# Index operations in halves, one row-blend batch, a near search to distance 5, and half of one sweep's search by VectorE's maxima

## The reference

```
center = einsum('nchw,oc->nohw', feature, w_center)          # 2 channels
step   = relu(einsum('nchw,oc->nohw', feature, w_step))      # 2 channels
prob   = sigmoid(einsum('nchw,oc->nohw', feature, w_prob))   # 1 channel
offset = center * step
th = minimum(round(gh + offset[0]), h - 1); tw = minimum(round(gw + offset[1]), w - 1)
tgt    = mod(th * w + tw, h * w)
sample = grid.at[tgt].set(grid)       # scatter: the last pixel that aims at a target wins
sampled = bilinear sample of feature at sample's coordinates (on whole pixels up to rounding)
proped = sampled * prob + feature * (1 - prob)
out    = feature * prob + proped * (1 - prob)
```

## The kernel before

| sweep | mixing | tabling | indices |
|---|---|---|---|
| 0 | | 0 | |
| 1 | | 1 | 0 |
| 2 | 0 | 2 | 1 |
| 3 | 1 | 3 | 2 |
| 4 | 2 | | 3 |
| 5 | 3 | | |

## Time and profile before

### The profile page before, as it was taken

One profiled execution on the slowest core, in us unless ns is written; L12 is line 12 of the kernel. 1 busy time (PEld: TensorE's weight loads), 2 busy tenths in 40 slices (PEclk: granted clock), 3 DMA queues, 4 the chain that ended last, 5 costly groups with the idle time before them and its releaser, 6 DMA issues. The chain is left out here.

```text
span 8694.0 us, 95812 instructions
## 1 busy us (share of the span) xinstructions
PE 6551.5 (75%) x26980; PEld 3016.8 (35%) x26980; DVE 5132.8 (59%) x11678; ACT 3770.3 (43%) x7426; POOL 4294.5 (49%) x8828
## 2 busy tenths in 40 slices
PE   5885675557657899579996787679996774688888
PEld 2332232223223444234552333234442332233333
DVE  3333355355754433555558885477778982566666
ACT  5664434323223444233330233456661654455555
POOL 3556866444343345443431443564452644566665
PEclk8997788768878999789999888789998786788888
DMA  4785545755456677555551377665551554676676
GB/s 177 285 296 185 201 167 203 193 175 191 143 142 213 243 281 277 188 183 188 196 207 60 136 240 217 204 178 177 177 179 53 177 176 121 191 221 221 217 222 200
DMA packets 489245, 1673.92 MB, mean 193 GB/s; under 512 B 119580, under 2 KB 140347, under 8 KB 421396
## 3 DMA queue, kind: packets, MB, share of 16 engines
q1 hardware_dynamic: 214092, 827.29, 30.9%
q10 hardware_dynamic: 210152, 764.05, 23.0%
q0 software_dynamic: 64480, 76.57, 4.8%
HBM read 949.99 MB, written 727.71 MB: 193 GB/s over the span
## 5 line engine op out<-in xcount | busy, mean ns | idle before, releaser
L1056 DVE TENSOR_TENSOR ps<-ps,arena 128x400 f32<-128x400 f32 x1600 | 928.4, 580 | 2178.1 <-PE ps L1170 1058.7
L1006 POOL TENSOR_TENSOR arena<-arena 128x32 f32<-128x32 f32 (+8 forms) x3358 | 968.8, 329 | 2497.4 <-PE ps L1193 1752.4
L1162 PE MATMUL ps<-arena,minus 128*128 128x400 f32 x3200 | 1692.4, 614 | 484.5 <-DVE arena L1058 359.0
L1318 ACT ACTIVATE arena<-ps 128x400 f32<-128x400 f32 x1600 | 800.8, 501 | 2584.7 <-PE ps L1156 968.5
L1193 PE MATMUL ps<-arena,w_conv 128*10 128x400 f32 x3200 | 1367.7, 535 | 284.1 <-ACT arena L1252 114.0
L1206 PE MATMUL ps<-ident,arena 128*128 128x128 f32 x5000 | 870.6, 320 | 615.6 <-ACT arena L1268 370.2
L1136 POOL DMA_INDIRECT arena<-table,gidx x800 | 903.8, 1130 | 829.4 <-PE ps L1179 570.0
L1252 ACT ACTIVATE arena<-ps 10x400 f32<-10x400 f32 x1600 | 785.2, 492 | 1119.2 <-PE ps L1193 1004.6
L1268 ACT ACTIVATE arena<-ps 128x512 f32<-128x512 f32 (+1 forms) x1400 | 731.8, 550 | 914.8 <-PE ps L1206 671.2
L1170 PEld LDWEIGHTS ps<-ident,arena 100*128 100x128 f32 x6400 | 779.6, 155 | 797.4 <-issue 643.4
L1136 POOL DMA_INDIRECT arena<-table,arena x800 | 810.0, 1013 | 480.0 <-issue 233.7
(11 more groups left out here) (210 smaller groups left out, 6313.6 us busy)
## 6 DMA issues: line engine op xcount, KB each, us to landing
arena<-x SPq DMA_DIRECT2D x200, 1600.0 KB
arena<-table SPq DMA_DIRECT2D x400, 800.0 KB
table<-arena ACTq DMA_DIRECT2D x400, 512.0 KB
y<-arena ACTq DMA_DIRECT2D x100, 1600.0 KB, 14.2
arena<-y SPq DMA_DIRECT2D x100, 1600.0 KB
out<-arena ACTq DMA_DIRECT2D x100, 1600.0 KB
table<-arena ACTq DMA_DIRECT2D x200, 576.0 KB
conv<-arena ACTq DMA_DIRECT2D x800, 31.2 KB
```

What stands on the lines that cost most here:

```text
L1006: last = E.tensor_tensor(tmp[:, :, at:at + size], cols[:, :, y + to:end + to:step], cols[:, :, y:end:step], ALU.subtract)
L1056: V.tensor_tensor(d, d, g, ALU.mult).then_inc(s_mix, 1)
L1162: nc.tensor.matmul(ps[:, 4 + r % 2, 0:W], minus[:, :], tile(t)[:, r * W:(r + 1) * W], start=True, stop=False)
L1318: nc.scalar.activation(gate[r % 2], ps[:, 6 + r % GB, 0:W], ACT.Copy).then_inc(s_gcopy, 1)
```

## The change

Four things are changed, and the paces with them.

1. *Halves.* In sweeps that mix (2, 3, 4) each whole-map piece of parts (1) and (4) becomes two pieces on 1600 elements (`pieces`, `cuts` = 2). Sweep 1 keeps whole pieces.
2. *Batches.* NEARBY becomes a list by tabled unit: 8 for units 0 and 1, tabled in sweeps 0 and 1, and 4 for units 2 and 3. With 8, no tile has two batches.
3. *Distance.* R of layer 1 is 5 and not 6: 121 offsets in place of 169.
4. *Search of unit 2 (sweep 3).* TensorE's sum is formed for two of the four row pairs only. For the other two VectorE compares into a float16 value i + 1 and takes the maximum with the running result in SBUF. Each step is one `found`, one compare for the other half and one maximum, two steps to a piece (`held` = 2).
5. *Pace* becomes 1.15 in sweeps 3 and 4, so about every seventh slot takes two pieces.

```diff
-NEARBY = 4
+NEARBY = [8, 8, 4, 4]
-REACH = [1, 6]
+REACH = [1, 5]
...
-        htmp = [part(W) for _ in range(NEARBY)]
+        htmp = [part(W) for _ in range(NEARBY[-1])]
...
+        htmp += [again(gates_at[0] - (a + 1) * W, W) for a in range(2)] + gate
...
+            PAIRED, held = (2, 2) if u == 2 else (BROWS // 2, HELD)
+            beside = [again(BPX // 2 + a * W, 2 * W, NB, F16).rearrange("p (r w) -> p r w", w=W) for a in range(2)]
...
+                def pieces(op, name=None):
+
+                    for a in range(cuts):
+                        size = BROWS // cuts
+                        note(op(slice(a * size * W, (a + 1) * size * W), slice(a * size, (a + 1) * size)), name)
+                        yield
+                        dve.wait_ge(s_v, n[0])
...
-                yield from piece(V.scalar_tensor_tensor(s0m, s0m, 0.0, c0m, ALU.max, ALU.mult))
+                yield from pieces(lambda c, r: V.scalar_tensor_tensor(s0m[:, c], s0m[:, c], 0.0, c0m[:, c], ALU.max, ALU.mult))
...
-                for a in range(BROWS // 2):
+                shared = u == 2
+                if shared:
+                    yield from piece(V.memset(near[:, BPX // 2:], 0.0))
+                for a in range(PAIRED):
                     for i in range(OFFSETS):
...
+                        if shared:
+                            b, h = a + 2, beside[i % 2]
+                            src = halo[:, j + RMAX - R + 2 * b:j + RMAX - R + 2 * b + 2, RMAX - R + e:RMAX - R + e + W]
+                            if c >= 2:
+                                dve.wait_ge(s_v, n[0] - 2)
+                            note(V.tensor_scalar(h, src, float(i + 1), float(i + 1), ALU.is_equal, ALU.mult))
+                            dve.wait_ge(s_v, n[0])
+                            to = m3(near)[:, 2 * b:2 * b + 2, :]
+                            note(V.tensor_tensor(to, to, h, ALU.max))
-                        if i % HELD == HELD - 1 or i == OFFSETS - 1:
+                        if i % held == held - 1 or i == OFFSETS - 1:
                             yield
...
-                vector, scalar, tensor, gpsimd, born = indices(u_idx)
+                vector, scalar, tensor, gpsimd, born = indices(u_idx, 2 if mixing else 1)
...
-                            if int((slot + 1) * pace) > int(slot * pace):
+                            for _ in range(int((slot + 1) * pace) - int(slot * pace)):
                                 next(work, None)
...
-        sweep(3, 1, 3, 2, spell=3)
-        sweep(4, 2, None, 3)
+        sweep(3, 1, 3, 2, pace=1.15, spell=3)
+        sweep(4, 2, None, 3, pace=1.15)
```

More of the change, by code:

```diff
@@ L96, with batches @@
 GROUPS = len(TURNED) * TILES + len(LATE)
-def batches(t):
+def batches(t, most):
     left, done = list(INNER[t]), []
@@ L134, in counted @@
 def counted(marks, u, t):
-    return u * sum(marks) + sum(marks[:t])
+    return sum(map(sum, marks[:u])) + sum(marks[u][:t])
 def constants():
@@ L472, in vector @@
[L472 to L499, removed]
@@ L500, in vector @@
-                yield from piece(V.tensor_tensor(c0m, c0m, c1m, ALU.subtract))
+                yield from pieces(lambda c, r: V.tensor_copy(parts[0][:, c], z[:, c]))
+                yield from pieces(lambda c, r: V.tensor_tensor(z[:, c], z[:, c], parts[0][:, c], ALU.subtract))
+                yield from pieces(lambda c, r: V.tensor_copy(parts[1][:, c], z[:, c]))
+                yield from pieces(lambda c, r: V.tensor_tensor(z[:, c], z[:, c], parts[1][:, c], ALU.subtract))
+                yield from pieces(lambda c, r: V.tensor_copy(parts[2][:, c], z[:, c]), "gate")
@@ L504, in vector @@
+                yield from pieces(lambda c, r: V.tensor_scalar(z[:, c], z[:, c], -1.0, 1.0, ALU.mult, ALU.add))
                 step(V.scalar_tensor_tensor(s1m, s0m, 1.0, z, ALU.add, ALU.mult), "far")
@@ L632, in vector @@
                 yield
[L635 to L639, removed]
@@ L640, in vector @@
-                yield from piece(V.scalar_tensor_tensor(m3(s0m), grows, float(W), gcols, ALU.mult, ALU.add))
-                yield from piece(V.scalar_tensor_tensor(c1m, c1m, -float(R * W + R), s0m, ALU.add, ALU.add))
-                yield from piece(V.scalar_tensor_tensor(c1m, near, 0.0, c1m, ALU.is_gt, ALU.mult))
+                yield from pieces(lambda c, r: V.tensor_scalar(c0m[:, c], near[:, c], -0.5, 1.0 / SIDE, ALU.add, ALU.mult))
+                yield from pieces(lambda c, r: V.tensor_scalar(c0m[:, c], c0m[:, c], 0.5, MAGIC, ALU.subtract, ALU.subtract))
@@ new lines, in vector @@
+                yield from pieces(lambda c, r: V.tensor_scalar(c0m[:, c], c0m[:, c], MAGIC, None, ALU.add))
+                yield from pieces(lambda c, r: V.scalar_tensor_tensor(c1m[:, c], c0m[:, c], -float(SIDE), near[:, c], ALU.mult, ALU.add))
+                yield from pieces(lambda c, r: V.scalar_tensor_tensor(c1m[:, c], c0m[:, c], float(W), c1m[:, c], ALU.mult, ALU.add))
+                yield from pieces(lambda c, r: V.scalar_tensor_tensor(m3(s0m)[:, r], grows[:, r], float(W), gcols[:, r], ALU.mult, ALU.add))
@@ L643, in vector @@
+                yield from pieces(lambda c, r: V.scalar_tensor_tensor(c1m[:, c], c1m[:, c], -float(R * W + R), s0m[:, c], ALU.add, ALU.add))
+                yield from pieces(lambda c, r: V.scalar_tensor_tensor(c1m[:, c], near[:, c], 0.0, c1m[:, c], ALU.is_gt, ALU.mult))
                 yield from blanks(2)
                 dve.wait_ge(s_farld, (u + 1) * 16 * 2)
-                yield from piece(V.tensor_tensor(c1m, c1m, s1m, ALU.max))
-                yield from piece(V.tensor_scalar(c0m, c1m, 0.0, None, ALU.is_equal))
@@ L648, in vector @@
-                yield from piece(V.scalar_tensor_tensor(c0m, s0m, 1.0, c0m, ALU.add, ALU.mult))
-                yield from piece(V.scalar_tensor_tensor(c1m, c1m, -1.0, c0m, ALU.add, ALU.add))
+                yield from pieces(lambda c, r: V.tensor_tensor(c1m[:, c], c1m[:, c], s1m[:, c], ALU.max))
+                yield from pieces(lambda c, r: V.tensor_scalar(c0m[:, c], c1m[:, c], 0.0, None, ALU.is_equal))
+                yield from pieces(lambda c, r: V.scalar_tensor_tensor(c0m[:, c], s0m[:, c], 1.0, c0m[:, c], ALU.add, ALU.mult))
```

114 lines of the change are left out of this document (66 added, 48 removed).

## The result

The changed kernel takes **8617.86 us** (median of 12 runs, 8592.42 to 8661.19), the kernel before 8697.5 us in the same session (12 runs, 8675.2 to 8715.12). The ratio is **0.9913, 95% interval 0.9895 to 0.9931**: faster by 0.9%, where 1.3% was forecast. The profiled span fell from 8694.0 to 8616.1 us.

A forecast was written before the change was run, and what follows sets the result against it. It took TensorE to bound index-free and near-search tiles, VectorE whole-piece tiles and sweep 4's picks. Terms -36 -30 -39 -24 +86 -32 -57 +10 +10 = -112 from 8696 gave 8584, forecast 8585 us, range 8465 to 8695.

The forecast's parts named there:

- batches: Sweeps 0 and 1: one batch removes ScalarE's waits between two batches, -36 us (28 and 8).
- halves: Sweeps 2, 3 and 4: half pieces let row mixing keep TensorE's pace; -30, -39 and -24 us.
- search and distance together: Sweeps 3 and 4: shared search with distance 5 -57 us, fewer searches in sweep 4 -32, its added far-list round +86.
- picks +10: Sweep 4's picks at pace 1.15: excess over base tiles goes from 48 to 59 us, +10; sweep 3 about 0.
- waits +10: Sweeps 3 and 4: six empty pieces cover only 5.2 slots, in three places each; +5 us per sweep.
- VectorE takes TensorE's place as the bound of sweep 3's search: Sweep 3's search: VectorE needs 31 us a tile against TensorE's 29.3; 36 us at 90% filling with waits.
- The 8 us of sweep 1: Sweep 1: part of ScalarE's 18.2 us wait between batches credited as saved, 8 us, bounds 0 and 18.
- perhaps 1 over: Sweep 2's half-piece tiles: 8.5 tiles each perhaps 1 us over a base of 30, 8 us against 32 before.
- latency, not VectorE's load, sets them: Piece tiles: sign that the prediction is wrong, if they stay at 37 us.
- The later pieces in sweep 2 only move the eleven tiles with VectorE's column blend: Sweep 2: the mark comes at slot 169 instead of 116, which only shifts those tiles; no cost charged.
- The third round: Sweep 4's far list: distance 5 needs three rounds instead of two, +86 us, bounds 80 and 90.
- 13.7 tiles at 36: Sweep 3's search: 126 pieces over 13.7 tiles of 36 us, plus 16 for row blends, 509 us in all.

The follow-up runs named there:

- u_shared: Changed kernel with all four row pairs of unit 2 searched by TensorE's sums alone; 8317.76 us, ratio 0.9935 to the kernel before.
- u_pace: Changed kernel with pace 1 (one piece a slot) in sweeps 3 and 4; 8235.98 us, ratio 0.9844 to the kernel before.
- best1: Changed kernel with distance 5 for unit 2, 6 for unit 3, pace 1 in sweep 3 and 1.05 in sweep 4; 8487.77 us, ratio 0.9764.

## Why the prediction was right, and where its sizes were off

The forecast of 8585 us lay 33 us below the median, inside its range, and its direction and most of its mechanisms hold. That the number came so near is in part luck, as the terms show, against what undoing each part measured (by the ratios; in brackets by the sweeps of single profiles):

| term | forecast | measured |
|---|---|---|
| batches | -36 | -36 (-26) |
| halves | -93 | -54 (-77) |
| search and distance together | -57 - 32 + 86 = -3 | -18 - 14 = -32 (-38) |
| pace: picks +10, waits +10 | +20 | +58 (+67) |
| sum | -112 | -64 (-74) |

The measured terms sum to within 16 us of the -80 of the medians, which is well inside their spread. A miss of 38 us on pace and one of 39 on halves (16 by the sweeps) were set off in part by 29 us too little for the search, and that last figure is no larger than its own spread by the ratios; the sweeps give 35.

*Bound.* That VectorE takes TensorE's place as the bound of sweep 3's search, and stays the bound of sweep 4's pieces and picks, was right. The step (1.17 us), the maximum (576 ns), the search tile (36.5 us), sweep 4's piece tile (28.3 us) and its pick tile (32.3 us, by the working 32.35) came out as forecast. But the trade of one bound for the other left the search tile where TensorE alone would have had it at this pace (36.4 us in u_shared), so the maxima gave 18 us, which their spread of 19 doesn't tell from none.

*Batches.* Right in sweep 0 (28 us forecast, 26 to 32 by the profiles), where the wait that was named is gone. The 8 us of sweep 1 did not come: ScalarE now waits for GpSimd's blend, which the prediction had named as the stage's bound, in place of VectorE, and 0 was the end of the range that held.

*Halves, over-credited.* The fixed cost was right: a piece of 1600 takes 1.82 us, by the prediction's 1.041 and 152 ns 1.818. The step that failed is "perhaps 1 over" the base in sweep 2. The tiles took 33.1 us where 31 were set, 17 us over 8 tiles, and the tile behind them that waits for the code's DMA took 58.9 us for 51.5. These two are the whole shortfall of 24. The same two in sweep 3 are 7 x 2.8 = 20 and 60.7 for 47.0. A cause is seen in part. The tile in which row blends begin, the third of the sweep, takes 42.5 and 45.2 us, which leaves 31.8 and 32.5 for the others on average: 11 of the 17 us are that one tile. In the eight tiles of sweep 2 VectorE stands idle for 24.3 us until ScalarE has scaled the neighbour rows (L1331), a wait for which the working had no term of its own. Whether that wait is the excess isn't shown. The named failure sign, "latency, not VectorE's load, sets them", came true at 33 us in place of 37: VectorE is busy 72% in these eight tiles of sweep 2, TensorE 77% at 0.82, and neither is full. The clock did not pass 0.9 either. In sweep 4, where VectorE stays full (91%), the arithmetic of load came out.

*"The later pieces in sweep 2 only move the eleven tiles with VectorE's column blend."* True, and they cost the same, 402 us in tiles 15 to 25 before and 405 in tiles 22 to 32 after.

*Distance.* The third round was right (+77 to +80 for +86). Under-credited was the search: -51 in sweep 4 for -32, and in sweep 3, where no round is added, -53 of distance and -14 to -18 of maxima against -57 for both.

*Pace, under-charged.* This is the largest miss. The prediction counted it for sweep 4's picks (+10) and six waits (+10), and called the rest of the search "13.7 tiles at 36", without setting it against 16 tiles at 32. By the price of a tile pushed out (23.25 less 9.2 us) two tiles of sweep 3's search alone are worth 28; the traces give 21. The cover of a late wait shrank as well, as charged (+5): that tile of sweep 3 took 45.3 us, 33.8 in u_pace and 36.2 in best1 at pace 1.

## What to carry to other kernels

When a side job runs in the slots of a main loop and its engine is the bound there, a faster pace isn't worth anything: the same work takes nearly the same time and covers fewer of the main loop's rows. Pace the side job so that it ends with the loop, and put a stall that can't be hidden at a boundary that drains anyway (12 us here, less than the pace itself). Where a cut (here the search distance) trades a fixed price in rounds for work saved, count the rounds for each data set by itself: 5 was right for one pair, and for the other 6 was better by 2 to 29 us of its sweep.

## What the runs showed of the hardware that was not expected

*The same code is 17% faster in one sweep in the other group of runs.* Sweep 5, which this change doesn't touch, in the changed kernel and in u_shared:

```profile
7351.00:8616.00 1265.00, 1064.60 (x4389) 460.67 (x4388) 834.40 (x1593) 646.33 (x1195) 789.72 (x784) 0.86 0.68 213
```

```profile
7247.00:8300.00 1053.00, 966.91 (x4397) 428.57 (x4397) 843.79 (x1600) 655.24 (x1195) 799.41 (x788) 0.96 0.80 256
```

VectorE, ScalarE and GpSimd have the same busy time. TensorE's busy time is 98 us longer at a granted clock of 0.86 for 0.96, and its idle time 114 us longer. Both groups have tiles of 20.5 us; the slower one scatters up to 34.5. What starts the gaps isn't settled by these runs, nor is it whether the chip makes the difference. It is why a kernel is only set against the kernel before of its own group.

*The parity of a float16 offset doesn't matter to the compare.* About half of the 121 windows of the search begin on an odd element; odd and even ones both have a median of 364 to 365 ns (L544 above, 132 even and 110 odd). 800 elements in 364 ns, less the 152 ns of fixed cost, are 3.8 elements a ns.

*The two engines disturb each other both ways, and more where pieces run.* In the search VectorE loses 0.12 us a step to GpSimd, as shown above. GpSimd's adds of the column blend (L1015 before) in the eight piece tiles of sweep 2, after the change:

```profile
L1036 POOL TENSOR_TENSOR arena<-arena 128x32 f32<-128x32 f32 (+8 forms) x172 | 75.0, 480 | 0.6
```

It took 799 ns beside whole pieces and 278 beside none; beside halves it takes 480, somewhat over the 400 forecast. The Trainium skill, "SBUF — State Buffer", section "SBUF: two separate sides", calls the shared port pair an exclusive lock held for the whole instruction; the trace agrees in direction, since beside pieces of half the length the extra fell from 521 to 202 ns.
